# Mixer and experts of a two-layer AdaLN network: maxima, router logits and key-value sums as full-width products, a new job order, and experts' rows in five buffers

## What is computed

```
h   = layernorm(x) * (1 + ca) + sa
qf, kf = elu(q) + 1, elu(k) + 1               # 16 heads of 16
kv  = kf^T v  per head;  k_sum = sum of kf     # "key-value sums"
x   = x + ga * ((qf kv) / (qf k_sum)) @ wo
h   = layernorm(x) * (1 + cb) + sb
attn = softmax(q k^T / 4)                      # 16 query heads, 4 key heads, 512 keys
src = rmsnorm(h + attn v @ ow)
logits = src @ gate_w                          # 8 experts
p   = sigmoid(logits); take the best 2, rank rows within each expert, drop over capacity
y   = sum over the 2 of weight * gelu(src @ w1[e]) @ w2[e]
x   = x + gb * rmsnorm(src + y)
```

## Time and profile before

| what | value |
|---|---|
| median of 3 runs | 3275.32 us (3271.12 to 3281.46) |
| profiled execution | 3295.55 us, span 3293.8 us |
| mean granted TensorE clock | 0.972 |
| busy share of the span | PE 93%, DVE 66%, ACT 48%, POOL 36% |
| L2827 row maxima | 1024 of 683 ns |
| L3380 and L3409 score products | 1024 each |
| L2445 exponentials | 1024 of 595 ns |
| L3423 weighing | 2048 records |
| L4128 and L4140 experts' products | 1136 records each |
| DMA | 337 MB, mean 102 GB/s |

### The profile page before, as it was taken

One profiled execution on the slowest core, in us unless ns is written; L12 is line 12 of the kernel. 1 busy time (PEld: TensorE's weight loads), 2 busy tenths in 40 slices (PEclk: granted clock), 3 DMA queues, 4 the chain that ended last, 5 costly groups with the idle time before them and its releaser, 6 DMA issues. The chain is left out here.

```text
span 3293.8 us, 55752 instructions
## 1 busy us (share of the span) xinstructions
PE 3056.6 (93%) x18230; PEld 1911.0 (58%) x18230; DVE 2188.0 (66%) x6629; ACT 1590.7 (48%) x3518; POOL 1202.1 (36%) x1522
## 2 busy tenths in 40 slices
PE   7899999999998995899999999999998859998897
PEld 3566767767765663344444444444443338887786
DVE  7777777777772224778888888888887732445455
ACT  3556565555551113476666666666665521111111
POOL 2123232232244113234444444444443234444445
PEclk9999999999999998899999999999999979999998
DMA  8110010010113971212222222222222128888885
GB/s 271 5 49 25 24 48 24 25 47 24 48 61 116 319 243 44 65 56 74 75 75 75 75 75 75 75 75 75 75 75 72 46 93 218 223 235 222 213 228 148
DMA packets 269343, 337.23 MB, mean 102 GB/s; under 512 B 43951, under 2 KB 218658, under 8 KB 269104
## 3 DMA queue, kind: packets, MB, share of 16 engines
q1 hardware_dynamic: 240112, 296.62, 29.4%
q0 software_dynamic: 28464, 34.71, 4.8%
q10 hardware_dynamic: 544, 3.15, 0.2%
HBM read 225.77 MB, written 113.95 MB: 103 GB/s over the span
## 5 line engine op out<-in xcount | busy, mean ns | idle before, releaser
L2827 DVE TENSOR_REDUCE negmax<-psum 128x1 f32<-128x512 f32 x1024 | 667.0, 683 | 164.6 <-PE psum L3380 149.2
L2445 ACT ACTIVATE pT<-psum 128x512 f32<-128x512 f32 x1024 | 576.0, 595 | 294.2 <-PE psum L3409 200.7
L3380 PE MATMUL psum<-k_stack,q_stack 96*128 96x512 bf16 x1024 | 358.6, 389 | 21.1 <-DVE negmax L2827 16.7
L3409 PE MATMUL psum<-q_stack,k_stack 99*128 99x512 bf16 x1024 | 361.1, 384 | 18.1 <-ACT pT L2445 10.5
L3994 POOL DMA_INDIRECT src_rows<-ye,place x142 | 223.3, 1573 | 330.8 <-DVE place L4030 126.0
L940 ACT ACTIVATE probs<-probs,negmax 128x256 f32<-128x256 f32 x512 | 252.8, 495 | 137.6 <-DVE negmax L1032 133.8
L4011 ACT ACTIVATE actT_x<-psum 128x512 f32<-128x512 f32 x142 | 84.8, 597 | 485.2 <-PE psum L4128 478.5
L3423 PE MATMUL psum<-pT,v_tile 128*32 128x512 f32 x2048 | 269.1, 609 | 1.0 <-ACT pT L2445 1.0
L4128 PE MATMUL psum<-xT_x,w_x 128*128 128x256 f32 x1136 | 263.6, 386 | 0.0
L4140 PE MATMUL psum<-w_x,actT_x 128*128 128x256 f32 x1136 | 256.6, 379 | 0.0
L1032 DVE CUSTOM_DVE_ANT_0 probs<-psum,band_mask 128x256 f32<-128x256 f32 x512 | 181.4, 420 | 104.6 <-PE psum L1296 104.1
(11 more groups left out here) (400 smaller groups left out, 5708.9 us busy)
## 6 DMA issues: line engine op xcount, KB each, us to landing
w_x<-in_L_ffn_w_dram SPq DMA_DIRECT2D x142, 512.0 KB, 4.4
w_e<-in_L_ffn_w_dram SPq DMA_DIRECT2D x46, 1024.0 KB, 7.4
q_stacks<-q_part SPq DMA_DIRECT2D x192, 128.0 KB
q_stack<-q_stacks SPq DMA_DIRECT2D x64, 384.0 KB, 4.4
padded<-w_e SPq DMA_DIRECT2D x32, 650.0 KB, 6.1
xe<-padded SPq DMA_DIRECT2D x71, 260.0 KB
gate_rows<-mods SPq DMA_DIRECT2D x66, 256.0 KB, 3.5
x<-in_L_attn_x_dram SPq DMA_DIRECT2D x16, 512.0 KB, 8.7
```

The costliest lines, as they stand in the source:

```text
L2445: act.activation(pT[:, 4 * (s % 2) + r, :], bank(m, 2 + n % 2), ACT.Exp, scale=float(DHQ) ** -0.5)\
L2827: dve.tensor_reduce(negmax[:, p // REP, h:h + 1], bank(m, max_bank(b, 16 * g + p)), AX.X, ALU.max, negate=True).then_inc(max_read, 1)
L3380: pe.matmul(bank(m, max_bank(b, 16 * g + p)), q_stack[0:K_SCORE, h, t * P:(t + 1) * P], k_stack[0:K_SCORE, g, :], start=True, stop=True).t ...
L3409: pe.matmul(bank(m, 2 + n % 2), k_stack[:, g, kc * P:(kc + 1) * P], q_stack[:, REP * g + r, :], start=True, stop=True).then_inc(sT_done, 1)
```

## The change

Five parts. First, the maxima: the three parts of a group lie in one tile of 96 columns (48 used, the rest zero), one transpose takes all of them, ScalarE copies 48 x 128, and three DMAs (one per part, 16 pieces of 256 B) write them out. Second, the key-value sums: 8 products with 128 stationary and 132 moving columns; VectorE picks the same blocks out of the wider result. Third, the logits: `gate_w` is spread to 32 columns by GpSimd once, TensorE multiplies it as stationary side with 128 rows moving, four products beside each other in 32 columns each; ScalarE copies the result, TensorE transposes it back, and the exponential reads that. Fourth, the jobs in all five bodies have a new order. Fifth, experts' rows lie in five buffers and are loaded one tile earlier. Several small counters are merged into `consts`.

```diff
-        max_part = sb("max_part", [P, NT, REP, 3], BF16)
-        maxT = sb("maxT", [3 * REP, 2, S], BF16)
+        max_part = sb("max_part", [P, 2 * NMP], BF16)          # NMP = 3 * REP * NT = 48
+        max_parts = max_part[:, 0:NMP].rearrange("p (j h t) -> p t h j", j=3, h=REP)
+        maxT = sb("maxT", [NMP, 2, P], BF16)
...
             def max_rows(b, g):
                 sp.wait_ge(maxT_ready, b * HKV + g + 1)
-                for h in range(REP):
-                    sp.dma_start(q_stack[K_SCORE:K_FULL, REP * g + h, :], maxT[3 * h:3 * h + 3, g % 2, :])\
-                        .then_inc(max_in[g], 16)
+                for j in range(3):
+                    sp.dma_start(q_stack[K_SCORE + j:K_SCORE + j + 1, REP * g:REP * (g + 1), :]
+                                 .rearrange("j h (t n) -> j (h t) n", t=NT),
+                                 maxT[REP * NT * j:REP * NT * (j + 1), g % 2, :]).then_inc(max_in[g], 16)
...
             # SyncE body: store_keys(b+1) ahead of max_rows(b, 2); load_h2_rows(b+1), load_rows(b+3)
             # ahead of max_rows(b+1, 1); store_src(b-1) last
...
+            def copy_logits(b):
+                act.wait_ge(logits_done, b + 1)
+                act.activation(logitT[:, :], bank(m, RB)[:, 0:P], ACT.Copy).then_inc(logitT_ready, 1)
...
             def key_values_sum(b):
                 for c in range(C):
                     for t in range(NT):
-                        for j in range(P // HPAIR):
-                            g = c * (P // HPAIR) + j
-                            mm = pe.matmul(bank(m, LB)[HPAIR * j:HPAIR * (j + 1), c * (HPAIR + 1):(c + 1) * (HPAIR + 1)],
-                                           k_exp[:, t, HPAIR * g:HPAIR * (g + 1)], v_one[:, t, g, :],
-                                           start=(t == 0), stop=(t == NT - 1))
+                        mm = pe.matmul(bank(m, LB)[:, c * GRAM:(c + 1) * GRAM], k_exp[:, t, c * P:(c + 1) * P],
+                                       v_one[:, t, c * (P // HPAIR):(c + 1) * (P // HPAIR), :]
+                                       .rearrange("p g n -> p (g n)"), start=(t == 0), stop=(t == NT - 1))
...
             def transpose_max(b, g):
-                for t in range(NT):
-                    mm = pe.transpose(bank(m, IB).bitcast(BF16)[0:3 * REP, t * P:(t + 1) * P],
-                                      max_part[:, t, :, :].rearrange("p h j -> p (h j)"), m.ident_bf[:, :])
-                mm.then_inc(maxT_done, 1)
+                pe.transpose(bank(m, IB).bitcast(BF16)[0:2 * NMP, 0:P], max_part[:, :], m.ident_bf[:, :])\
+                    .then_inc(maxT_done, 1)
...
             def logits(b):
-                for t in range(NT):
-                    for c in range(C):
-                        mm = pe.matmul(bank(m, RB)[:, t * E:(t + 1) * E], srcT[:, c, t * P:(t + 1) * P],
-                                       gate_w[:, c, :], start=(c == 0), stop=(c == C - 1))
+                for c in range(C):
+                    for t in range(NT):
+                        mm = pe.matmul(bank(m, RB)[VW * t:VW * (t + 1), 0:P], gate_cols[:, c, :],
+                                       srcT[:, c, t * P:(t + 1) * P], start=(c == 0), stop=(c == C - 1))
                 mm.then_inc(logits_done, 1)
+
+            def transpose_logits(b):
+                pe.wait_ge(logitT_ready, b + 1)
+                pe.transpose(bank(m, RB)[:, P:2 * P], logitT[:, :], m.ident[:, :]).then_inc(logit_rows, 1)
...
             # VectorE body, start: values, add_load(b-2), row_max(b,1,8), read_rank(b-2), second_stats(b+1,1),
             # row_max(b,1,9..11) (before: read_rank between row_max 14 and 15)
             # TensorE body, start: scoresT 0,1; weigh(b-1,15); scoresT 0,2; max 8; scoresT 0,3;
             # transpose_hidden 0; scoresT 1,0 1,1; count(b-2); max 9, 10; weigh 0 (before: count ahead of max 14)
...
+    XB = 5                                           # experts_block; x_in and weights keep WB = 3
-        xe = sb("xe", [P, WB, RT, ROW])
+        xe = sb("xe", [P, XB, RT, ROW])
...
+            sp.wait_ge(xT_done, 1)
+            load_rows(WB)
             for i in range(NTILEX):
+                if i + WB + 1 < NTILEX:
+                    sp.wait_ge(xT_done, i + 2)
+                    if i:
+                        sp.wait_ge(weight_ready, 4 * i)
+                    load_rows(i + WB + 1)
                 if i + WB < NTILEX:
                     e = number(i + WB, E - 1)
-                    sp.wait_ge(xT_done, i + 1)
-                    sp.wait_ge(weight_ready, 4 * i + 4)
-                    load_rows(i + WB)
                     sp.wait_ge(up_done, 2 * i + 2)
                     load_up(i + WB, e)
```

More of the change, by code:

```diff
@@ L2100, in body @@
             def body(b, par, part):
+                if part(1):
+                    store_keys(b + 1)
                 if part(0):
@@ L2300, in body @@
                 if part(-2):
[L2301 removed]
+                    scatter(b - 2, par, 2)
                 if part(2):
@@ L2309, in body @@
                     normalise_first(b + 3)
+                if part(-2):
+                    scatter(b - 2, par, 3)
                 if part(2):
                     add_branch(b + 2, 0)
+                if part(-2):
+                    scatter(b - 2, par, 4)
+                    scatter(b - 2, par, 5)
+                if part(2):
                     add_branch(b + 2, 1)
+                if part(-2):
+                    scatter(b - 2, par, 6)
+                    scatter(b - 2, par, 7)
             for b in range(-3, -1):
@@ L3026, in body @@
                     values(b, par)
+                if part(-2):
+                    add_load(b - 2)
+                if part(0):
+                    row_max(b, 1, 8)
+                if part(-2):
+                    read_rank(b - 2)
+                if part(1):
+                    second_stats(b + 1, 1)
+                if part(0):
+                    row_max(b, 1, 9)
+                    row_max(b, 1, 10)
+                    row_max(b, 1, 11)
+                if part(1):
+                    second_variance(b + 1, 1 - par)
+                if part(-1):
+                    normalise(b - 1, 0)
+                if part(0):
+                    row_max(b, 1, 12)
                 if part(3):
@@ L3547, in body @@
                 if part(0):
-                    scoresT(b, 0, 1)
-                if part(-1):
-                    weigh(b - 1, 15, 1 - par)
+                    scoresT(b, 1, 0)
+                    scoresT(b, 1, 1)
+                if part(-2):
+                    count(b - 2)
+                if part(0):
+                    max_scores(b, 1, 9)
+                    max_scores(b, 1, 10)
+                    weigh(b, 0, par)
                 if part(2):
@@ L3729, in body @@
                     max_scores(b + 1, 0, 6)
+                    max_scores(b + 1, 0, 7)
+                if part(0):
+                    scoresT(b, 11, 1)
+                if part(2):
+                    numerators(b + 2, 0)
+                if part(1):
+                    max_scores(b + 1, 0, 8)
+                    queries_keys(b + 1, 2)
+                if part(0):
+                    scoresT(b, 11, 2)
+                if part(1):
+                    max_scores(b + 1, 0, 9)
                 if part(0):
@@ L3761, in body @@
                 if part(1):
-                    max_scores(b + 1, 0, 12)
+                    max_scores(b + 1, 0, 14)
+                    max_scores(b + 1, 0, 15)
+                if part(-1):
+                    transpose_src(b - 1, 1 - par, 1)
                 if part(0):
                     scoresT(b, 13, 1)
+                if part(2):
+                    numerators(b + 2, 3)
+                if part(0):
                     scoresT(b, 13, 2)
                 if part(1):
-                    max_scores(b + 1, 0, 13)
+                    max_scores(b + 1, 1, 0)
+                if part(-1):
+                    logits(b - 1)
                 if part(0):
```

628 lines of the change are left out of this document (297 added, 331 removed).

## The result

The changed kernel takes 3284.32 us (median of 20 runs), the kernel before 3276.51 beside it: ratio 1.0022, interval 1.0011 to 1.0032. The forecast was 3265; the change makes the kernel slightly slower. A later session gave 1.0044 (1.0027 to 1.0060).

A forecast was written before the change was run, and what follows sets the result against it. TensorE's own work was taken to bound the mixer, scatter landings the late experts' tiles. Terms -5 (batches), -1.3 (last batch) and -4 (experts) took 3295.6 to 3285.3 us, scaled to 3265; range 3236 to 3290.

The forecast's parts named there:

- Sums, +1.00 a batch: Mixer, TensorE's key-value sums: 0.79 us in narrow form becomes 1.79 in 8 full-width products, +1.00 us a batch.
- 0, at worst +2: Mixer's start: gate columns, zeros and the constants' counter lie beside loads and cost 0, at worst 2 us.
- Logits, -0.97: Mixer, TensorE's router logits: 1.70 us becomes 0.73 including switches and the new transpose, -0.97 us a batch.
- Last batch -1.3: Mixer's last batch, logits uncovered at half clock: 3.6 us becomes 2.3, so -1.3 us once.
- Maxima, -0.77: Mixer, TensorE's transposes of the maxima: one of 96 columns replaces four of 12 per group, -0.77 us a batch.
- The whole effect on the bounding engine's work: Mixer, TensorE: maxima, sums, logits and order together give -0.34 us a batch, -5 us over 15 batches.
- Order and adjacent weighings, +0.40 and 0 for waits: Mixer's new job order: separated weighings cost +0.40 us a batch; TensorE's 3.2 us of waits stay, counted 0.
- rival D: Mixer: new order makes VectorE and TensorE wait for each other, value copies 83.5 us or more apart, 3303 us; chance 0.18.
- Mixer in sum: Mixer as a whole: -5 us over 15 batches and -1.3 in the last batch, -6.3 us.
- Experts' rows, -4 (ends 0 and -38, other sign +11): Experts' stage: earlier row loads win the middle stretch's 4 us; ends 0 and -38; bursts of three loads could cost +11.
- the chain is untouched: Experts' late tiles: the change leaves the chain of scatters alone, so the 34.5 us row wait only changes its name.
- Base: Starting point: profiled execution of 3295.6 us with late experts' tiles at 8.29 us; forecast scaled to the median 3275.3.

The follow-up runs named there:

- rows5: Kernel before with only the changed kernel's experts' block (five row buffers, rows loaded earlier, three loads issued together): ratio 1.0046, 14.5 us slower.
- before_again: Kernel before, unchanged, timed and profiled a second time: ratio 0.9996 to itself, profiled span 3260.3 us.
- rows5_gate: Kernel before with five row buffers, but a tile's loads still wait for VectorE's weighing of the tile just multiplied: ratio 1.0260.
- after_again: Changed kernel, unchanged, timed and profiled a second time: ratio 1.0044 to the kernel before, profiled span 3283.0 us.

## Why the prediction failed, step by step

- **Sums, +1.00 a batch:** 1.00 measured. But their price was counted in overlapped batches only. The first two batches have no cover, and the wide sums ran there near half clock: some 5 us more, missed ("0, at worst +2" for the set-up was the only term for the start).
- **Logits, -0.97:** -1.04. Last batch -1.3: from the first product at 2656.74 to the exponential at 2658.74 it is 2.0 us, against 3.62, so -1.6.
- **Maxima, -0.77:** 0.68 in TensorE's pitches, 0.2 in the period. "The whole effect on the bounding engine's work" did not reach the period; the likely reason is that TensorE also waits for VectorE's maxima.
- **Order and adjacent weighings, +0.40 and 0 for waits:** by difference -0.50 - (1.00 - 1.04 - 0.20) = -0.26 a batch. The maxima's part was measured in the old order and the other two in the new one, so this difference also holds what they do to each other. The new order is at most a small gain; rival D did not happen in the mixer (81.7, not 83.5 and more).
- **Mixer in sum:** -6.3 forecast, -5 measured (interval -10 to 0). That they are close is in part luck: the start cost 5 to 7, the batches gave 7.5 and the last batch 1.6, which makes -2 to -4.
- **Experts' rows, -4 (ends 0 and -38, other sign +11):** +14.5 (rows5). This is the step that failed and that reversed the sign of the forecast. The wait's change of name was right, its new place too, and "the chain is untouched" was wrong: the chain's landings depend on when loads go out. I had this as a mishap of 0.3 us a landing; it was 0.34 over 70 tiles against the second profile of before, or 24 us, some 15 by the timed runs. Why the mean landing grew by this much is argued above, not shown. The point to ask was what paces the loads once TensorE's waits are gone.
- **Base:** the profiled execution had long landings and the stall. Its late pace of 8.29 us I took for the kernel's; an ordinary execution has 307 us for 631 records, 7.8 a tile, and so less to win.
- The range, 3236 to 3290, held the time, though for no reason that it was drawn for: a loss had 0.18, mostly for waits in the mixer (D) that did not come, while a loss in the experts' stage stood only as an end of +11.

## What to carry to other kernels

When a chain of scatter-adds, each waiting for the one before to land, sets the pace, a load's moment counts more than its lead: look at what goes out beside a scatter (here 3.7 or 7.4 us a landing by that) before giving loads more buffers, and at what a removed wait was pacing. Price a wider product also where it runs alone and at half clock. Take two profiles of the kernel before when the one at hand is off its own median.

## What the runs showed of the hardware

- A scatter-add of 128 rows landed in 2.7 us at best and 8.9 at worst (both in before_again). In the changed kernel it was 4.79 or 8.45 us from a tile's second scatter to the next tile's first, with one load of weights beside it or five loads. Gating the loads on a step that itself waits for a landing cost 87 us (rows5_gate).
- Moving stores and source loads by one or two tiles, with the same bytes and work, won 16 us (0.9950).
- 16 product records of 128 x 132 took 1.8 us among other work at full clock, 2.04 alone at full clock (after_again), and 2.96 and 3.61 at a mean granted clock of 0.66 and 0.55. 64 narrow ones on a quarter of the array each took 0.70, 0.76 (both at full clock) and 1.10 at 0.50.
